# Two PSUM banks for scores, four for dense products, and a query bias added by VectorE, in a two-layer attention and expert kernel

## What is computed

```python
x = x + attention0(layernorm(x), ctx, mask, with biases b_q, b_k, b_v, b_o)   # 16 heads of 16
x = x + ffn(layernorm(x), ternary W1, W2)                                      # 256 -> 1024 -> 256
x = x + attention1(layernorm(x), ctx, masked by length)                        # no biases
x = x + moe(layernorm(x))      # 8 auto-encoders; the one with the least loss picks an adapter
# attention: query = q @ w_q + b_q; scores = query . key; softmax over keys; times value; @ w_o
```

## Time and profile before

| what | value |
|---|---|
| median of 3 runs | 1706.56 us (1704.66 to 1708.15) |
| profiled execution, its own time | 1703.62 us |
| its span in the trace | 1701.8 us |
| share of the span in which PE is busy | 91% |
| granted TensorE clock, mean | 0.966 |

### The profile page before, as it was taken

The page is one execution under the profiler, slowest core; times in us unless marked ns, Lnnn a source line. Parts: engine busy times, 40 slices in busy tenths (PEclk is TensorE's granted clock), DMA queues, the critical chain, the costliest instruction groups (busy, mean ns, idle before and its releaser), DMA issues.

```text
span 1701.8 us, 43831 instructions
## 1 busy us (share of the span) xinstructions
PE 1548.6 (91%) x15136; PEld 1266.4 (74%) x15136; DVE 1272.1 (75%) x5086; ACT 920.0 (54%) x2465; POOL 1096.1 (64%) x1198
## 2 busy tenths in 40 slices
PE   2567999999999999999999999999999999999865
PEld 1356787788878887878887878788888778877654
DVE  6446778888777788887777888877777888876542
ACT  0133556655555566655555566555555665565532
POOL 4377777666767776667667766666677666666200
PEclk7689999999999999999999999999999999999977
DMA  8446565655566655565666555556666555643311
GB/s 195 76 76 94 78 102 95 99 94 97 95 105 97 106 94 96 96 92 92 104 109 94 96 97 100 91 94 103 105 92 104 95 96 95 95 77 55 60 25 30
DMA packets 286212, 157.23 MB, mean 92 GB/s; under 512 B 38820, under 2 KB 281640, under 8 KB 285992
## 3 DMA queue, kind: packets, MB, share of 16 engines
q1 hardware_dynamic: 285992, 154.44, 55.7%
HBM read 111.36 MB, written 41.96 MB: 90 GB/s over the span
## 4 chain that ended last, share of the span: by engine, by line
PE 46%; DVE 25%; DMA 12%; SPq 7%; issue 6%; ACT 2%; POOL 1%; DVEq 0%; ACTq 0%; POOLq 0%
DMA qs<-scr 11%; DVE dif L924 8%; DVE dump L858 7%; PE psD L1234 7%; PE psD L1223 6%; SPq L375 4%; PE psD L1202 4%; PE psS L1165 4%; PE psD L1268 4%; PE psD L1139 4%; PE psD L1215 3%; PE psD L1244 3%; PE psX L1177 3%; SPq L359 3%; PE psV L1190 2%
## 5 line engine op out<-in xcount | busy, mean ns | idle before, releaser
L629 ACT ACTIVATE pT<-psX 128x512 f32<-128x512 f32 x512 | 305.0, 596 | 285.9 <-PE psX L1177 285.0
L522 POOL TENSOR_TENSOR pT<-pT,keep 128x512 f32<-128x512 f32 x256 | 318.2, 1270 | 5.6 <-ACT pT L629 5.6
L507 POOL TENSOR_SCALAR xn<-xr,mv,rstd 128x256 f32<-128x256 f32 x256 | 310.6, 1221 | 10.1
L481 POOL TENSOR_SCALAR veps<-mv 128x2 f32<-128x2 f32 x128 | 28.9, 226 | 405.6 <-DVE mv L803 403.1
L1165 PE MATMUL psS<-ks,qs 65*128 65x128 f16 x2048 | 203.8, 222 | 67.7 <-DMA qs<-scr 48.2
L850 DVE TENSOR_REDUCE mx<-psS 128x4 f32<-128x512 f32 x256 | 173.9, 679 | 118.8 <-PE psS L1165 118.8
L858 DVE CUSTOM_DVE_ANT_0 dump<-psS,bias 128x128 bf16<-128x128 f32 x1024 | 233.7, 283 | 33.2 <-PE psS L1165 30.6
L673 ACT ACTIVATE dif<-dif 128x256 f32<-128x256 f32 x512 | 208.0, 410 | 50.8 <-DVE dif L924 48.9
L924 DVE SCALAR_TENSOR_TENSOR dif<-psD,bd2s,xT 128x256 f32<-128x256 f32 x512 | 213.6, 471 | 21.3 <-PE psD L1244 21.3
L1177 PE MATMUL psX<-qs,ks 67*128 67x128 f16 x2048 | 200.2, 220 | 32.1 <-DMA qs<-mrows 18.0
L1165 PEld LDWEIGHTS psS<-ks,qs 65*128 65x128 f16 x2048 | 136.9, 99 | 114.7 <-issue 69.9
(11 more groups left out here) (103 smaller groups left out, 2975.0 us busy)
## 6 DMA issues: line engine op xcount, KB each, us to landing
scr<-packed SPq DMA_DIRECT2D x128, 256.0 KB, 2.5
ks<-scr SPq DMA_DIRECT2D x256, 128.0 KB, 5.3
qs<-scr SPq DMA_DIRECT2D x256, 128.0 KB, 4.4
adapter<-in_adapters SPq DMA_DIRECT2D x64, 192.5 KB, 3.7
xr<-in_x SPq DMA_DIRECT2D x32, 256.0 KB, 2.9
ctxT<-in_ctx SPq DMA_DIRECT2D x32, 256.0 KB, 3.0
qs<-mrows SPq DMA_DIRECT2D x512, 2.0 KB
out_y<-xr SPq DMA_DIRECT2D x32, 256.0 KB, 6.9
```

The costliest lines, as they stand in the source:

```text
L507: nc.gpsimd.tensor_scalar(xn[:, XN[s], b], xr[:, p % NX, b], mv[:, s, b, 0:1], rstd[:, s, b:b + 1], ALU.subtract, ALU.mult).then_inc(norme ...
L522: nc.gpsimd.tensor_tensor(blk, blk, keep[:, p % 2, j // 4].unsqueeze(1).to_broadcast([P, 4, P]), ALU.mult).then_inc(masked.sem, 1)
L629: nc.scalar.activation(pT[:, j], X[:], ACT.Exp, scale=SCALE).then_inc(exp_done[l].sem, 1)
```

## The change

The bank S becomes two, `SB[0]` and `SB[1]`, used in turn by j; the dense products get four banks instead of five, with a new table `BANKS`. The two bias matmuls of `queries(0, p)` go, and DVE gets `bias_q(p)`: two operations that add bias times `anyb` to the query product in PSUM, in place. ACT's `high(0, 0, p)` waits for it instead of for `queries(0, p)`. The bias is loaded as a column, so the work at the start that split it in bf16 parts goes, with two of its three loads. The semaphore of the maxima's landing is one for each batch. Every engine's list is written anew; no other operation is added or left out.

```diff
-END = BODY * (NP - 1) + 83
+END = BODY * (NP - 1) + 78
 BANKS = (
-    ("F1_0", "q1", "O0", "F1_3", "T0", "rec1", "F1_1", "hd0", "up"),
-    ("v0", "rec4", "rec3", "k1", "hd1", "down", "T3"),
-    ("loss", "rec7", "rec0", "F1_2"),
-    ("k0", "rec6", "T2", "v1", "O1"),
-    ("rec2", "cnt", "T1", "rec5", "F2", "q0"),
+    ("k0", "F1_2", "rec1", "rec6", "hd0", "rec4"),
+    ("T1", "O1", "cnt", "T0", "rec2", "F1_0", "rec5", "down", "T3", "O0", "hd1"),
+    ("v0", "rec3", "k1", "q1", "q0", "T2", "F2"),
+    ("F1_1", "F1_3", "v1", "rec7", "rec0", "loss", "up"),
 )
-        S = pb("psS")
+        SB = [pb(f"psS{k}") for k in range(2)]
-        DB = [pb(f"psD{k}") for k in range(5)]
+        DB = [pb(f"psD{k}") for k in range(4)]
 # high, on ACT
-                (k_ready if j else q_ready)[l].done(act, p)
+                (k_ready[l] if j else q_ready[1] if l else q_biased).done(act, p)
 # on DVE, before low(0, 0, p)
+            def bias_q(p):
+                q_ready[0].done(dve, p)
+                any_row.done(dve, p)
+                for m in range(KD):
+                    part = bank["q0"][:, m * T:m * T + T]
+                    ins = nc.vector.scalar_tensor_tensor(out=part, in0=anyb[:], scalar=bqs[:, m:m + 1], in1=part,
+                                                         op0=ALU.mult, op1=ALU.add)
+                ins.then_inc(q_biased.sem, 1)
 # start of DVE: nine operations on bqr, bq_part, bq_rest go
-            nc.vector.tensor_copy(bq_part, bq_ld).then_inc(bq_steps, 1)
...
 # queries, on PE
-                    if l == 0:
-                        ins = nc.tensor.matmul(dst[:, m * T:m * T + T], bqr[:, m * P:m * P + P], anyb[0:65],
-                                               start=False, stop=True)
 # scores, on PE
-                claim("S", max_done[l], p, j)
+                claim(f"S{j % 2}", max_done[l], p, j)
+                S = SB[j % 2]
 # a few of the calls that moved: DVE
-                for p in at(t, 48):
-                    split_max(1, p, 1)
...
                 for p in at(t, 47):
                     maximum(1, p, 7)
+                    split_max(1, p, 1)
```

More of the change, by code:

```diff
@@ L279, in build @@
         stacked = [[sem(f"stacked{l}{k}") for k in range(2)] for l in range(2)]
-        m_landed = [sem(f"m_landed{l}") for l in range(2)]
+        m_landed = [[sem(f"m_landed{l}{b}") for b in range(PB)] for l in range(2)]
         gathered = sem("gathered")
@@ L404, in _ @@
             for t in range(FIRST, END):
-                for p in at(t, 82):
-                    store(p)
-                for p in at(t, 51):
-                    maxima(1, p, 1)
-                for p in at(t, -11):
+                for p in at(t, -14):
                     load(p)
@@ L555, in _ @@
                     apply_mask(p, 0)
+                for p in at(t, -8):
+                    mask_bias(p)
                 for p in at(t, 8):
@@ L558, in _ @@
                 for p in at(t, 24):
+                    h_lows(p, 0)
+                for p in at(t, 25):
                     h_lows(p, 1)
@@ L576, in _ @@
                     apply_mask(p, 5)
+                for p in at(t, 28):
+                    add_bias(1, p)
                 for p in at(t, 13):
@@ L700, in _ @@
                     copy_xT(2, p)
+                for p in at(t, 35):
+                    high(1, 0, p)
                 for p in at(t, 51):
@@ L733, in _ @@
                     copy_xT(0, p)
-                for p in at(t, 24):
-                    high(1, 1, p)
                 for p in at(t, 25):
-                    relus(p, 2)
                     h_highs(p, 1)
@@ L994, in _ @@
                     differences(p, 5)
+                for p in at(t, -13):
+                    statistics(0, p)
                 for p in at(t, 3):
                     maximum(0, p, 3)
[L997 to L998 removed]
                 for p in at(t, 36):
                     low(1, 0, p)
[L1001 to L1004 removed]
                 for p in at(t, -12):
@@ L1009, in _ @@
                 for p in at(t, 68):
+                    differences(p, 6)
+                for p in at(t, 4):
+                    maximum(0, p, 4)
+                for p in at(t, 21):
+                    x_lows(p)
+                for p in at(t, 69):
                     differences(p, 7)
-                for p in at(t, 20):
-                    x_lows(p)
                 for p in at(t, 5):
@@ L1045, in _ @@
                     statistics(3, p)
+                for p in at(t, -5):
+                    bias_q(p)
                 for p in at(t, 43):
@@ L1053, in _ @@
                     maximum(1, p, 4)
-                for p in at(t, 12):
-                    turn_out(0, p, 0)
                 for p in at(t, 76):
                     add_up(p)
+                for p in at(t, 13):
+                    turn_out(0, p, 0)
+                for p in at(t, 29):
+                    add_ffn(p)
                 for p in at(t, 45):
@@ L1395, in _ @@
                     reconstruct(p, 0)
+                for p in at(t, 15):
+                    mix(0, p, 1)
                 for p in at(t, 47):
                     scores_t(1, p, 1)
-                for p in at(t, 15):
-                    mix(0, p, 1)
 _ARGS = [
```

266 lines of the change are left out of this document (119 added, 147 removed).

## The result

| | before | after |
|---|---|---|
| median | 1705.61 us (1703.15 to 1708.15, 4 runs) | 1652.66 us (1646.31 to 1655.75, 4 runs) |
| ratio, 95% interval | | 0.9685 [0.9652, 0.9718] |
| profiled execution, span | 1703.62, 1701.8 us | 1655.75, 1654.0 us |
| granted clock, mean | 0.966 | 0.965 |

The change makes the kernel 3.1% faster; 2.4% was forecast. The page of the changed kernel, which answers to the earlier trace rows: its span, the busy times, and the shares of the chain that ended last.

What follows compares the result with a forecast made beforehand. PE's work plus two DMA waits, ending a chain through DVE, was taken as the bound. Rounds: -0.23 - 0.65 - 0.44 = -1.32 us, 27 give -35.6; start -6; 1662 profiled, median 1665 us (2.4% faster), range 1646 to 1694.

Steps and rivals of the forecast that it cites:

- The chain: Layer 1's last scores through DVE and SP's DMAs to its first scores: DVE's 18.0 us become 16.1, plus 9.75.
- The wait for `qs<-mrows`: PE, before layer 0's first transposed scores, for the maxima's four DMAs: goes wholly, 0.65 us a round.
- The wait for `qs<-scr`: PE, before layer 1's first scores, for the queries' DMA from DRAM: 0.84 us a round falls to 0.4.
- I cost it at nothing: bias_q's 0.9 us ahead of ACT's high: covered on PE by mix(0, p, 0); without cover 0.3 to 0.9 a round.
- The claims of banks: Four dense banks instead of five: new neighbours cost no wait; bank 2's claim by values(0, p) has 0.7 us cover.
- The start: First rounds: bias parts gone, two banks S, earlier keys' write; together -7.4 us at best, taken as -6.
- The second bank: At the start, DVE alone sets the pace of four or five scores of the first pair: -3.5 us.
- The end: Behind the steady rounds: taken as it is, no change costed.
- A+: Rival: queries' DMA lands 0.4 us sooner, no wait is left, the start gives more: 1648 us; chance 0.14.
- A: Main case: the steady rounds and start gain as summed, 1665 us (1655 to 1680); chance 0.58.
- B: Rival: queries' DMA landing depends on traffic, not issue, so its wait stays: 0.35 us a round, 1693 us; chance 0.18.
- C: Rival: with four dense banks a bank becomes PE's wait, slower, 1720 us at 2.7 us late; chance 0.10.

Runs made afterwards that it cites:

- E5: Changed kernel with maximum(0, p, 4) and differences(p, 6) ahead of split_max(0, p, 0) on DVE again: 1699.11 us, ratio 0.9953 to the kernel before.
- E2: Changed kernel with the query bias back on PE as two matmuls a pair, no bias_q: 1651.08 us, ratio 0.9658 to the kernel before.
- E9: Changed kernel with the keys' write behind the four DMAs of layer 0's second maxima on SP again: 1656.40 us, ratio 0.9693.
- E1: Changed kernel with one bank S for scores again, everything else as changed: 1791.57 us, ratio 1.0487 to the kernel before.
- E12: Changed kernel with two PE swaps, reconstruct(p, 3) ahead of scores_t(1, p, 6), and ACT's exps(0, p, 5)/high(0, 0, p) swap except for the first five pairs: 1639.21 us.
- E3: Kernel before with two banks S and four dense banks, old order except losses behind the mix on PE: 1742.88 us, ratio 1.0211.
- E4: Kernel before with only the bias moved to DVE (bias_q): 1720.65 us, ratio 1.0075.
- E6: Kernel before, one bank S, with two DVE moves: differences(p, 6) behind split_max(0, p, 0), split_max(1, p, 1) ahead of differences(p, 0): 1744.25 us, ratio 1.0216.

## Why the prediction was right, point by point

**The chain.** Right, and shown. The maxima were forecast 16.1 us behind layer 1's last scores and came after 16.47; SP's part was forecast at 9.75 us and took 9.39. The two errors cancel: 25.85 forecast, 25.86 measured in this round, so that the sum fits this closely is luck. E5 shows that the order on DVE makes it.

**The wait for `qs<-mrows`** goes wholly: right. **The wait for `qs<-scr`**: "a wait of 0.4 us stays in place of 0.84". About 0.2 stays, since PE itself, costed at 25.5 us for this stretch, comes 0.2 us later by the new wait ahead of `turn(1, p)`.

**"I cost it at nothing"**, of `bias_q`: the step that failed. The cover, `mix(0, p, 0)` ahead of the transposed scores, did hold for the exponentials, but `a_relus` stands in the same queue of ACT, and `up` on PE has no cover for it: 0.27 us a round, a little more than the 0.23 that the matmuls gave back (E2). The size of `bias_q`, 0.9 forecast and 0.88 measured, was right, and the loss was under the 0.5 us that the prediction named as its limit. The DVE work was followed to its first reader on ACT and not to the call behind that.

**The claims of banks.** Right for the changed order, at nothing. One wait not on my list came, 0.20 us ahead of `turn(1, p)`, for POOL.

**The sum.** 1.32 us a round forecast, 1.20 measured: the three steady terms -0.23, -0.65 and -0.65, with +0.27 and +0.20, make -1.06, and the rest, 0.14, lies in calls that have other neighbours now. Over 24 rounds the forecast gives 31.7 us and the traces 28.9.

**The start.** The term was -6 us, and 12.9 were gone at the seventh pair (its key count came 8.7 us earlier, at 266.05, where 5 to 8 was forecast). So the range given was missed, and the parts fit less well than the total. E2 puts 1.8 us to the bias. The keys' write, which I had as "up to -2.6", is not seen to give more than 0.5 (E9). The second bank was costed at 3.5 us for the first pair: two banks in the old order make the first interval 2.7 us shorter (36.8 for 39.5), and one bank in the new order makes it 3.7 longer (39.9 for 36.2), of which 1.0 is an operation of `split_max(0, 0, 1)` held beside POOL (1.16 us for 0.18). So this term was a little high. The kernel before has that operation held too (1.19 us) and the changed one not, 1.0 us that was no term. My own sum of the gains was 7.4 at best; the other 5.5 us were not in it, and "slots of `queries` and masks moved, which I can't sum" stood there as a loss. By E1, 2.3 us of them are the new order in the second interval (40.5 for 42.8) without a second bank; which moves gave the others was not tried. Each kernel was traced once, and starts differ by a us or two without an edit's doing: from SP's write of the second pair's queries to its reading them back are 4.57 us in the changed kernel, 5.04 in E9 and 2.99 in E12.

**The end.** "I take as it is": off by 4.8 us in the last pair's scores of layer 1, and by 2.2 the other way behind them. Windows of these two stretches, before (the columns are those of the earlier trace rows, the seventh is the granted clock):

```profile
1621.60:1642.00 20.40, 17.04 (x81) 12.84 (x82) 8.27 (x19) 2.16 (x5) 3.38 (x4) 0.65 0.05 14
1642.00:1701.80 59.80, 37.29 (x243) 26.89 (x239) 22.42 (x67) 22.68 (x85) 3.38 (x4) 0.76 0.08 23
```

And with the change:

```profile
1576.40:1591.90 15.50, 13.99 (x80) 11.30 (x81) 7.15 (x16) 2.16 (x6) 3.38 (x4) 0.83 0.06 18
1591.90:1654.00 62.10, 38.03 (x244) 27.34 (x241) 22.42 (x67) 22.71 (x85) 3.38 (x4) 0.72 0.08 22
```

In the first stretch PE and DVE took turns on S before: PE stood 2.5 us in three waits for `maximum`, and has none with the change. Another 2.0 us are one call, `up`: 4.62 us from its start to the next before, 2.67 with the change, where the granted clock was 0.58 before (from 1631.6 to 1636.6, so 1.2 GHz for most of it) and 0.96 after (from 1581.4 to 1586.4). In the traces taken, every kernel with one bank S needs 4.3 to 4.9 us for this call and every kernel with two 2.67, so bank and clock come together, and no run parts them. The 2.9 us of E3 (the banks alone) and the 1.7 of E1 (the order alone) contain both as well: E4, with the old order and one bank, took 1.0 us less than the kernel before, at a clock of 0.74 for 0.65. Behind this stretch the engines' work is the same, and the clock was lower: 0.72 for 0.76. E9, whose lists differ from the changed kernel's on SP alone, took 57.8 us there at 0.80. So the 2.2 us go with the clock that an execution is granted, and nothing shows that they belong to the change.

**The rivals.** In size the result lies nearer to A+ (1648 us) than to the number given for A (1665), and within the range. But this is not A+'s doing: from the seventh pair to the last pair's first scores of layer 1 the traces differ by 32.3 us where A had 35.6, and the start gave 6.9 us more than A had, the end 2.6 more. The other 6 us of the distance from 1665 are the step to the median: 2.9 us above the profiled execution in the forecast, 3.1 below it in the result. Half of A+'s mechanism came as well: SP's part was 0.36 us shorter, where A+ had 0.4. B falls by E5. C does not happen in the changed order, but E3, the banks alone, is C; in E6, the DVE moves alone, the wait is at the one bank S. In both, an operation of DVE is held beside POOL, which was in none of the rivals. One bank was said not to matter in the steady part, since "PE still never stands for `maximum`"; E6 shows that this was true only because two other waits covered it, by 0.2 us.

## What to carry to other kernels

A wait that no view prints can still be the next bound: before removing a wait, measure how late the next producer is behind the same start, here DVE's maximum at 28.19 us against PE's 29.08. A resource and the order that uses it have to be changed together: the banks alone cost 2.1%, the moves alone 2.2%, and both with their order gain 3.1%. In both of the losing runs part of the loss is where POOL's long instructions fall on DVE's small ones, so a moved call has to be looked at for what runs beside it, too. When work moves to another engine, follow its delay through that engine's and its reader's whole queue, not only to the first reader.

## What was not expected of the hardware

A VectorE operation of 128x16 elements that takes 0.17 us took up to 1.20 beside POOL's `TENSOR_TENSOR` instructions of 128x512 elements, and ended 0.03 or 0.04 us behind them; in E6 this was 1.87 us of DVE's time in a round, in E3 1.2 in `split_max(0, p, 1)`. POOL's instructions on 128x2 elements did not show it. The two operations of `bias_q`, which read and write PSUM in place, took 0.49 us each (0.88 for the pair), where those of `differences`, which write SBUF, took 0.47 (0.83 to 0.87 for a pair): writing in place cost next to nothing. And the same PE call costs more or less by what follows it: `turn(2, p)`, start to start, took 0.44 us with scores behind it (before) and 0.59 with a reconstruction (after), `turn(1, p)` 0.46 with scores and 0.54 with a reconstruction (E12).
